# A decoder layer's second half: row additions cut in pieces and moved, the gates turned later, the expert biases as one fp16 product, and other fills

## What is computed

```
x = layernorm(x + self_attention(x) @ Wout.T + bout)      # causal, 16 heads of 32
x = layernorm(x + cross_attention(x, ctx) @ Wo + bo)      # 16 heads, 77 context rows
x = layernorm(x + experts(x))
# experts: logits = cos(x, centroids) + x @ w_route.T     (8 experts)
#          gates  = softmax over the two largest logits, 0 elsewhere
#          h = gelu(x @ w1[e] + b1[e]);  y = h @ w2[e] + b2[e]
#          result = sum over e of gates[e] * y            (all 8 experts are computed)
```

## Time and profile before

| | us |
|---|---|
| median of 3 runs (2581.89 to 2583.79) | 2583.78 |
| the profiled execution | 2584.22 |
| its span in the profile | 2582.4 |
| TensorE busy in the span | 2400.6 |
| VectorE, ScalarE, GpSimd busy | 1714.1, 1102.6, 1118.8 |

### The profile page before, as it was taken

One profiled execution on the slowest core, in us unless ns is written; L12 is line 12 of the kernel. 1 busy time (PEld: TensorE's weight loads), 2 busy tenths in 40 slices (PEclk: granted clock), 3 DMA queues, 4 the chain that ended last, 5 costly groups with the idle time before them and its releaser, 6 DMA issues. The chain is left out here.

```text
span 2582.4 us, 36273 instructions
## 1 busy us (share of the span) xinstructions
PE 2400.6 (93%) x13556; PEld 1007.0 (39%) x13556; DVE 1714.1 (66%) x3957; ACT 1102.6 (43%) x2066; POOL 1118.8 (43%) x404
## 2 busy tenths in 40 slices
PE   7999799999999999999846899999999999999998
PEld 3444223333333232323223454544545454454543
DVE  4433587777777777777125567767676776767665
ACT  4332156666666666666612232323323242332320
POOL 0000369999999999999931112111011211102100
PEclk9999799999999999999968899999999999999999
DMA  7864402122130303130040001010100101010000
GB/s 245 291 226 159 111 11 70 50 52 70 32 91 14 87 25 80 31 104 18 18 156 30 17 1 63 1 53 11 46 17 1 62 1 60 4 46 17 1 17 17
DMA packets 130443, 155.00 MB, mean 60 GB/s; under 512 B 19838, under 2 KB 98174, under 8 KB 129245
## 3 DMA queue, kind: packets, MB, share of 16 engines
q1 hardware_dynamic: 130269, 152.69, 19.2%
HBM read 99.96 MB, written 52.17 MB: 59 GB/s over the span
## 5 line engine op out<-in xcount | busy, mean ns | idle before, releaser
L762 ACT ACTIVATE probs<-st_ps 128x512 f32<-128x512 f32 (+3 forms) x1280 | 610.3, 537 | 327.1 <-PE st_ps L865 179.7
L637 POOL TENSOR_TENSOR total<-total,probs 128x2048 f32<-128x2048 f32 (+3 forms) x200 | 706.5, 3532 | 47.6 <-ACT probs L762 26.6
L804 DVE TENSOR_REDUCE seg_max<-s_ps 128x1 f32<-128x512 f32 x768 | 506.1, 685 | 136.0 <-PE s_ps L851 133.8
L851 PE MATMUL s_ps<-k_pair,q_pair 96*128 96x512 f16 (+3 forms) x1280 | 435.0, 355 | 25.9 <-DMA q_pair<-q_parts 11.4
L865 PE MATMUL st_ps<-q_pair,k_pair 98*128 98x512 f16 (+3 forms) x1280 | 434.4, 353 | 25.7 <-ACT probs L762 16.5
L1429 PE MATMUL fps<-x2T,w_p_hi 128*128 128x512 f16 x1024 | 317.3, 379 | 0.0
L1429 PE MATMUL fps<-w_p_hi,hT 128*128 128x512 f16 x1024 | 306.0, 380 | 0.0
L885 PE MATMUL o_ps<-probs,v_sb 128*32 128x512 f32 (+3 forms) x2560 | 303.0, 546 | 0.0
L808 DVE CUSTOM_DVE_ANT_0 s_ps<-s_ps,later 128x384 f32<-128x384 f32 (+3 forms) x512 | 249.2, 500 | 66.2 <-issue 66.2
L1133 POOL TENSOR_TENSOR rstd<-rstd,keep_power 128x4 f32<-128x4 f32 x24 | 26.1, 1086 | 538.7 <-DVE rstd L1254 538.7
L865 PEld LDWEIGHTS st_ps<-q_pair,k_pair 98*128 98x128 f16 x1280 | 123.3, 98 | 328.1 <-ACT probs L762 233.5
(11 more groups left out here) (164 smaller groups left out, 3401.8 us busy)
## 6 DMA issues: line engine op xcount, KB each, us to landing
k_pair<-k_parts SPq DMA_DIRECT2D x96, 128.0 KB, 4.5
q_pair<-q_parts SPq DMA_DIRECT2D x96, 128.0 KB, 5.1
x_raw<-xT_in SPq DMA_DIRECT2D x8, 1024.0 KB, 6.2
q_parts<-qk_out SPq DMA_DIRECT2D x32, 256.0 KB, 4.1
k_parts<-qk_out SPq DMA_DIRECT2D x32, 256.0 KB, 4.1
piece_raw<-w_in SPq DMA_DIRECT2D x8, 1024.0 KB, 9.1
v_rows<-v_out SPq DMA_DIRECT2D x32, 256.0 KB, 2.1
w_parts<-piece_cut SPq DMA_DIRECT2D x8, 1024.0 KB, 6.0
```

The costliest lines, as they stand in the source:

```text
L637: last = nc.gpsimd.tensor_tensor(summed[:, :, off:], other[:, :, off:], probs[:, k % NP, :, off:], ALU.add)
L762: nc.scalar.activation(probs[:, k % NP, h, off:], st_ps[:, p % (2 * NVU) % RING, off:], ACT.Exp, scale=SCALE).then_inc(exp_done.sem, 1)
L804: nc.vector.reduce_max(highest, s_ps[:, slot], AX.X).then_inc(s_read.sem, 1)
L851: nc.tensor.matmul(s_ps[:, slot, 0:width], q_pair[a][0:NR, c, h, j * P:(j + 1) * P], k_pair[a][0:NR, h, s * CH:s * CH + width], start=True ...
```

## The change

It has four parts, all in the second half.

1. **Row additions.** The addition of `bout` and that of `bo` are cut into 4 instructions of 128 x 512 each. `bout` is added in stage turn2 of the chunk before (behind the second norm, when the next x has been loaded), `bo` in the stages pv0 to pv3, one piece each.
2. **Gates.** The chain no longer turns the gates in stage gate. A unit `gate` stands behind h(0,0) and h(0,1) of the next pass and uses a bank of the units.
3. **Bias product.** VectorE writes the gates, times a scale, as high part, low part and high part again into 96 columns (`g_stack`); turned, they are an fp16 tile `gT` of 96 rows. `b2_stack` holds b2 as high, high and low part. A bias unit is one fp16 matmul of 96 rows instead of an fp32 product of 8 rows. At the start of the second half GpSimd clears the two stacks, ScalarE and VectorE fill `b2_stack`.
4. **New fills.** The table `PLAN` is changed, and there are 53 units instead of 52.

```diff
-    PLAN = [("out", 1), ("norm1", 2), ("turn1", 3), ("query", 1), ("scores0", 3), ("scores1", 7), ("scores2", 7),
+    PLAN = [("out", 1), ("norm1", 3), ("turn1", 6), ("query", 2), ("scores0", 2), ("scores1", 6), ("scores2", 7),
             ("scores3", 6), ("probs0", 0), ("probs1", 1), ("pv0", 1), ("probs2", 0), ("pv1", 1), ("probs3", 0),
-            ("pv2", 3), ("pv3", 1), ("out2", 6), ("norm2", 3), ("turn2", 2), ("route", 4), ("gate", 0)]
+            ("pv2", 2), ("pv3", 1), ("out2", 5), ("norm2", 3), ("turn2", 2), ("route", 4), ("gate", 0)]
...
-        UNITS += [("hidden", e, n) for n in range(2) if e < E]
+        UNITS += [("hidden", e, n) for n in range(2) if e < E] + [("gate", 0, 0)] * (e == 0)
...
-            def add_row(row, c):
-                nc.gpsimd.tensor_tensor(x1[:], x1[:], row[:].rearrange("p (a n) -> p a n", a=1).broadcast_to(
-                    [P, TT, D]), ALU.add).then_inc(c.sem, 1)
+            def add_row(row, j):
+                nc.gpsimd.tensor_tensor(x1[:, j], x1[:, j], row[:], ALU.add).then_inc(biased.sem, 1)
+
+            def bias_rows(n):
+
+                pool.wait_ge(x_loaded, 16 * (n + 1))
+                for j in range(TT):
+                    add_row(W["bout_bc"], j)
...
                 if stage == "out":
-                    pool.wait_ge(x_loaded, 16 * (chunk(i, u) + 1))
-                    add_row(W["bout_bc"], biased)
                     pool.wait_ge(varied.sem, at(varied, i, u, 0))
                     root(rstd[:], rooted, TT)
-                elif stage == "turn1":
-                    pool.wait_ge(c_ready.sem, at(c_ready, i, u, AT_T1 + TT - 1))
-                    add_row(W["bo_bc"], biased)
...
+                elif stage.startswith("pv"):
+                    g = int(stage[-1])
+                    pool.wait_ge(c_ready.sem, at(c_ready, i, u, AT_VAL[g]))
+                    add_row(W["bo_bc"], g)
...
+                elif stage == "turn2" and chunk(i, u) + 1 < NC:
+                    pool.wait_ge(normed.sem, at(normed, i, u, 2 * TT - 1))
+                    bias_rows(chunk(i, u) + 1)
...
+                elif kind == "gate":
+                    act.wait_ge(f_ready.sem, at(f_ready, i, u, f))
+                    act.wait_ge(f_ready.sem, at(f_ready, i, u, LAST_BIAS - NUNIT))
+                    nc.scalar.activation(gT[:], fps[0:GS, experts_slot(i, u, f)].rearrange("e (j n) -> e j n", j=TT),
+                                         ACT.Copy).then_inc(gate_read.sem, 1)
...
-                elif stage == "gate":
-                    pe.wait_ge(routed.sem, at(routed, i, u, 12))
-                    bank = chain_bank(i, u, AT_G)
-                    for j in range(TT):
-                        last = nc.tensor.transpose(bank[0:E, j * P:(j + 1) * P], gates[:, j], ident[:])
-                    last.then_inc(c_ready.sem, 1)
...
-                    pe.wait_ge(act_read.sem, at(act_read, i, u, nth(USES, AT_G) - act_read.per // 2))
-                    last = nc.tensor.matmul(bank, gT[u][:, j], W["b2_sb"][:], start=True, stop=True)
+                    pe.wait_ge(b2_ready, 1)
+                    pe.wait_ge(gate_read.sem, at(gate_read, i, u, 0))
+                    last = nc.tensor.matmul(bank, gT[:, j], b2_stack[:], start=True, stop=True)
+                elif kind == "gate":
+                    pe.wait_ge(routed.sem, at(routed, i, u, 15 - routed.per // 2))
+                    for r in range(TT):
+                        last = nc.tensor.transpose(bank[0:GS, r * P:(r + 1) * P], g_stack[:, r], ident[:])
```

More of the change, by code:

```diff
@@ L956, in chains @@
             + ["act"] * HG + (["act"] * HG + ["dve"]) * (NG - 1) + ["dve"] + ["dve"] * TT + ["dve"] * TT
[L957 removed]
+            + ["dve"])
     AT_OUT, AT_T1, AT_Q = 0, TT, 2 * TT
@@ L966, in chains @@
     AT_R = AT_T2 + TT
-    AT_G = AT_R + 1
     NUSE, CB, FB = len(USES), 4, 4
+    GP = 32
+    GS = 3 * GP
     UNITS = []
     for e in range(E + 1):
-        UNITS += [("hidden", e, n) for n in range(2) if e < E]
+        UNITS += [("hidden", e, n) for n in range(2) if e < E] + [("gate", 0, 0)] * (e == 0)
         UNITS += [("bias", 0, j) for j in range(TT) if e == 1] + [("expert", e - 1, j) for j in range(TT) if e > 0]
     NUNIT = len(UNITS)
-    F_USES = ["act" if kind == "hidden" else "dve" for kind, _, _ in UNITS]
-    assert 2 * NUSE % CB == 0 and 2 * NUNIT % FB == 0
-    PLAN = [("out", 1), ("norm1", 2), ("turn1", 3), ("query", 1), ("scores0", 3), ("scores1", 7), ("scores2", 7),
+    F_USES = [{"hidden": "act", "gate": "turn"}.get(kind, "dve") for kind, _, _ in UNITS]
+    GATE, LAST_BIAS = UNITS.index(("gate", 0, 0)), UNITS.index(("bias", 0, TT - 1))
+    PLAN = [("out", 1), ("norm1", 3), ("turn1", 6), ("query", 2), ("scores0", 2), ("scores1", 6), ("scores2", 7),
             ("scores3", 6), ("probs0", 0), ("probs1", 1), ("pv0", 1), ("probs2", 0), ("pv1", 1), ("probs3", 0),
-            ("pv2", 3), ("pv3", 1), ("out2", 6), ("norm2", 3), ("turn2", 2), ("route", 4), ("gate", 0)]
+            ("pv2", 2), ("pv3", 1), ("out2", 5), ("norm2", 3), ("turn2", 2), ("route", 4), ("gate", 0)]
     STAGES, FILL = zip(*PLAN)
@@ L1011, in chains @@
         gates_un = [sb(f"gates_un{a}", [P, TT, E], F32) for a in range(2)]
-        gT = [sb(f"gT{a}", [E, TT, P], F32) for a in range(2)]
+        g_hi = sb("g_hi", [P, TT, E], F16)
+        g_stack, gT = sb("g_stack", [P, TT, GS], F32), sb("gT", [GS, TT, P], F16)
+        b2_hi, b2_stack = sb("b2_hi", [GS, D], F16), sb("b2_stack", [GS, D], F16)
         cps = stack.enter_context(nc.psum_tensor("cps", [P, CB, CH], F32))
@@ L1029, in chains @@
         hi_ready = count("hi_ready", TT + NG + TT)
-        biased = count("biased", 2)
+        biased = count("biased", 2 * TT)
         summed, spread, varied = count("summed", 2 * TT), count("spread", 2 * TT), count("varied", 2)
@@ L1215, in experts, with split_b2 @@
                     act.wait_ge(h_lo.sem, at(h_lo, i, u, n - 2))
-                    nc.scalar.activation(hidden[:, n % 2], fps[:, (u * NUNIT + f) % FB], ACT.Gelu,
+                    nc.scalar.activation(hidden[:, n % 2], fps[:, experts_slot(i, u, f)], ACT.Gelu,
                                          bias=W["b1_sb"][:, n:n + 1], scale=UN).then_inc(gelu_done.sem, 1)
+                elif kind == "gate":
[3 more added lines that the diff above has]
+                                         ACT.Copy).then_inc(gate_read.sem, 1)
+            def split_b2():
+                act.wait_ge(zeroed, 2)
+                for r, dst in ((0, b2_stack), (GP, b2_stack), (2 * GP, b2_hi)):
+                    nc.scalar.activation(dst[r:r + E], W["b2_sb"][r:r + E], ACT.Copy, scale=WS).then_inc(b2_split, 1)
+            split_b2()
             run(act, program(chain, experts))
@@ L1227, in wait_product @@
                 dve.wait_ge(c_ready.sem, at(c_ready, i, u, k))
-                return cps[:, (u * NUSE + k) % CB]
+                return cps[:, chain_slot(i, u, k)]
             def lo_part(i, u, k, hi_index, dst, hi):
-                bank = cps[:, (u * NUSE + k) % CB]
+                bank = cps[:, chain_slot(i, u, k)]
                 if len(dst.shape) == 3:
@@ L1370, in experts @@
             def experts(i, u, f, kind, e, j):
-                bank = fps[:, (u * NUNIT + f) % FB]
+                bank = fps[:, experts_slot(i, u, f)]
                 q = u
+                if kind == "gate":
+                    return
                 if kind == "hidden":
@@ L1387, in experts @@
                 if kind == "bias":
-                    nc.vector.tensor_tensor(x2[q][:, j], bank, x2[q][:, j], ALU.add).then_inc(added.sem, 1)
+                    nc.vector.scalar_tensor_tensor(x2[q][:, j], bank, UN, x2[q][:, j], ALU.mult,
+                                                   ALU.add).then_inc(added.sem, 1)
                 else:
```

50 lines of the change are left out of this document (34 added, 16 removed).

## The result

The changed kernel takes 2601.85 us (median of 4 runs, 2599.37 to 2604.84), beside 2583.2 us of the kernel before: a ratio of 1.0073, 95% interval 1.0056 to 1.0091. It is slower by 0.7%, 4.9 us above the 2597 us of the prediction and within its range.

A forecast was written before the change was run, and what follows sets the result against it. TensorE's row of work with a few holes was taken to bound the kernel. Six looped passes +17, first pass +8, lead-in -9.4 and tail -2.2 were summed to +13.6: 2597 us as a median, range 2558 to 2618.

The forecast's parts named there:

- The new waits: TensorE waiting for banks of expert units: +1.9 us a looped pass in turn1, +10.3 in the scores stages.
- the replay: Engines' orders replayed from the lists with durations from the rows; gave the new waits in turn1 and the scores.
- The rivals in which the scores wait less or not at all: Scores stages: only covers count, 6.0 us a pass, 2562 us, chance 0.14; or no new wait, 2519 us, chance 0.08.
- The clock behind h(5,0): Low clock behind the 3.3 us wait ahead of h(5,0): half of 1.7 us taken, +0.8 a looped pass.
- -10.2: Gains of a looped pass together: bias product -3.3, gates -1.6, queries' wait -3.6, low clock behind it -1.7 us.
- the rival in which the clock falls more: Low clock in full behind the 3.5 and 3.3 us waits, and in turn1: 2619 us, slower; chance 0.10.
- The queries' wait: Turn1: `bo`'s addition holds VectorE's split of h(1,0); moving it removes the wait, -3.6 us, and low clock, -1.7, a looped pass.
- The other gains: Looped pass: bias product in fp16, four units from 4.2 to 0.9 us, -3.3; gates' transposes covered, -1.6 us.
- The gates' wait: Ahead of the gates' transposes: 1.6 us in each of seven passes goes, with 15.6 us of cover; 7.83 stood in the lead-in.
- The ends: Lead-in -9.4 us, with out products following the routing at 1424.6; tail -2.2 us.
- The first pass: First pass of the loop, lacking the queries' 3.6 us gain and the 1.7 of clock: +8 us.
- The table load: ScalarE in the scores: the replay used 1.28 us; the skill's 2.7 us would add some 20 us over seven passes.

The follow-up runs named there:

- Experiment 3: Changed kernel with one unit, h(2,0), moved from scores0 back to scores1: 2580.0 us, ratio 0.9987 to the kernel before.
- experiment 8: Changed kernel with x(0,0) moved from turn1 to behind the query products: 2594.62 us, ratio 1.0039 to the kernel before.
- experiment 1: Changed kernel with the old table of fills, norm1 getting one more unit for the gate unit: 2511.63 us, ratio 0.9721 to the kernel before.
- Experiment 9: Changed kernel with old fills, but `bo` added whole in turn1 again, `bout` in pieces: 2511.54 us, ratio 0.9716 to the kernel before.
- experiment 12: Kernel before with only `bout`'s addition cut into pieces in turn2: 2550.86 us, ratio 0.9864 to the kernel before.
- 4: Changed kernel with old fills, but `bout` and `bo` added whole in stages out and turn1 again: 2549.43 us, ratio 0.9867 to the kernel before.
- 11: Changed kernel with old fills, but `bout` added whole in stage out again, `bo` in pieces: 2531.91 us, ratio 0.9791 to the kernel before.
- experiment 6: Changed kernel with old fills, but the bias product in fp32 with 8 rows again: 2532.80 us, ratio 0.9800 to the kernel before.
- experiment 5: Changed kernel with old fills, but the gates' transposes in stage gate again, norm1 back at 2: 2536.78 us, ratio 0.9818 to the kernel before.
- 7: Changed kernel with old fills, but two expert units moved from scores0 into query: 2506.19 us, ratio 0.9698 to the kernel before.
- experiment 10: Changed kernel with h(5,0) moved from scores3 behind probs0 and h(5,1) to probs1: 2624.73 us, ratio 1.0160 to the kernel before.

## Why the prediction held, and where it did not

**The new waits: right, in place, cause and size.** Predicted +3.5, +1.1, +1.3, +1.1, +3.3 in the scores and +1.9 at x(0,0); the trace has 3.45, 1.07, 1.34, 1.06, 3.17 and 1.86. The releasers are the ones named. Experiment 3 shrinks the first two to 0.96 and 0.83 us, where the replay says 1.2 and 1.0, experiment 8 the one at x(0,0), experiment 1 all six. The rivals in which the scores wait less or not at all are out. The replay worked because it used every engine's own order and durations from rows, and counted from one event; a sum of covers alone would have given 6.0 us.

**The clock behind h(5,0): mis-sized, and not always there.** The prediction took half of 1.7 us for the half-clock stretch (1.2 GHz) behind the wait of 3.3 us. Every pass loses the whole 1.7: the first five behind that wait, the last two at the wait of 3.5 us ahead of x(1,3), where 2.8 us are lost and the next wait takes 1.06 of them back. The prediction had put nothing there, since the next wait would take up most of the loss; it takes back less than half. For a looped pass the terms add up: -10.2 + 1.9 + 10.1 + 1.7 = +3.5 against a measured +3.3, where the prediction had +2.8. No pass has both stretches, so the rival in which the clock falls more (2619 us) is out.

**The queries' wait: the sum right, the cause half wrong.** The step said that the 3.58 us come from the addition of `bo` in turn1, and go because `bo` moves. Experiment 9 has `bo` in its old place and no wait; experiment 12 moves only `bout`, and the wait and the half clock behind it go, 35 us in all. The chain of causes is one link longer. `bout`'s addition starts just before VectorE scales the third norm, and holds it: four instructions in 6.08 us, 1.92 us without it (experiment 12, at 1728.88). GpSimd's row for it in the kernel before, which the earlier trace rows leave out:

```profile
1735.01 4.50 POOL L1129 TENSOR_TENSOR keep_x<-keep_x,keep_bout_bc 128x2048 f32<-128x2048 f32 x1
```

VectorE catches up most of the 4.2 us, since without `bout`'s addition it waits for the out products instead, but not all. Counted from the first out product of the pass (1730.93 before, 1724.73 in experiment 12), `bo`'s addition starts at 20.12 us in both kernels, the split of h(1,0) at 20.20 before and at 19.05 without `bout`'s addition. These 1.15 us decide whether the split comes behind the addition or ahead of it. The row with the 6.08 us stood among the prediction's own rows and was not followed up. Both rows moved in this change, so the number came out right by luck.

| time, us | `bo` whole | `bo` in pieces |
|---|---|---|
| `bout` whole | 2549.4 (4) | 2531.9 (11) |
| `bout` in pieces | 2511.5 (9) | 2511.6 (1) |

The table (experiment numbers in brackets) shows it: `bo` costs some 17 to 20 us if `bout` has made VectorE late (17.5 by the medians, 20 by the ratios), and nothing if not. Here the traces agree with a rule of the Trainium skill, SBUF — State Buffer, section Who interferes with whom: what VectorE runs with at most one input in SBUF, outside its modes that use two ports, doesn't contend with GpSimd; in a mode with two ports it does, and whichever started first keeps the shared port pair for its whole instruction. `work<-cps,work` has one of its operands in PSUM and took 2.48 us for four beside the addition; `hT<-hidden` and `x<-x` have input and output in SBUF, started behind the addition, and were held. Which mode an instruction ran in, no row shows.

**The other gains: right.** A bias unit takes 0.22 us from start to start; experiment 6 gives 3.5 us for the product (predicted 3.3). The gates' wait is gone; experiment 5 gives 25 us for it with the stack's instructions, lead-in included. GpSimd's pieces took 1.27 us each where the prediction had 1.13, and held up nothing that TensorE waits for.

**The ends: within what the lead-in varies by.** The lead-in gave 7.5 us instead of 9.4. The out products follow the routing at 1424.1 as predicted (1424.6), but the first half had ended 1.6 us earlier, so the chain of the lead-in is itself 1.3 us longer than before. Neither difference can be read as an effect of the change: experiments 1, 3, 7, 8 and 10 have the same first half and lead-in as the changed kernel, and there the lead-in takes 101.5 to 104.6 us and begins between 1320.3 and 1324.7. The first pass is +7.2 (predicted +8), the last pass with the tail +1.2 (predicted +0.6, from +2.8 and -2.2). The prediction's terms as written add up to +13.4, not +13.6, which changes nothing in its 2597. Against that sum the spans differ by 15.9: five looped passes give 2.5 us more than predicted, the last 0.6, the lead-in 1.9, the first pass 0.8 less, and the shorter first half takes 1.6 off.

**The table load.** The replay's 1.28 us held in the changed kernel too (1932.63 above). The 2.7 us that the prediction cites from the Trainium skill, ScalarE: Activation LUTs, What ACT_TABLE_LOAD costs, are there for a whole switch: 1283 ns of load, which this trace agrees with, and the rest a drain behind it. Of a drain the trace shows nothing: from the end of the exponential (1932.61) to the start of the Gelu (1933.93) are 1.32 us, load included.

**What stays open.** Why the half clock follows the wait of 3.2 us in the changed kernel's first five passes and comes at that of 3.5 us in the last two, though both waits stand in all seven, and why two of three passes of experiment 8 have both, no run here tells. Nor was h(5,0)'s wait taken away by itself: experiment 10 uncovered another.

## What to carry to other kernels

Where in-order engines share a small ring of banks, replay the orders of all of them from the rows before moving a unit across a stage: the same code was 3.0% faster or 0.7% slower than before by its table of fills alone, and a unit moved away from a wait can be the cover of a longer one (experiment 10). Run a change of code and a change of order apart: here a gain of 72 us was hidden under a loss of 90. And where an instruction takes many times its usual duration, look for what made it late enough to meet the one that blocks it; here that was an earlier collision, in another stage, and moving that one away was enough.
